# First unit of a float32-split attention kernel: weight stages in other places, keys and queries before the last values, low parts put from ScalarE's queue, Wo split four tiles later

## The reference

```python
q, k, v = X @ Wq, X @ Wk, X @ Wv                    # 16, 8, 8 heads of 64
q = q * cos + rotate_half(q) * sin                  # and k likewise
att = softmax(where(causal, 50 * tanh(q @ k.T / 16 / 50), -inf))
x = layernorm(X + (att @ v) @ Wo)
...                                                 # per-row int8 quantisation of x
x = layernorm(x + ((q8 @ weight.T) * in_scale * w_scale + bias).astype(float16))
```

## Time and profile before

| what | us |
|---|---|
| median of three runs (1493.48 to 1496.95) | 1494.65 |
| the profiled execution | 1498.59 |
| its span in the profile | 1496.8 |
| PE busy in the span | 1327.0 |
| DVE, ACT, POOL busy | 1094.6, 847.4, 379.1 |

### The profile page before, as it was taken

How to read it: one execution, slowest core, us unless ns; L and a number is a source line. 1 busy time by engine, 2 the same in 40 slices (tenths; PEclk the granted TensorE clock), 3 DMA queues, 4 the chain that set the end, 5 groups by cost and what they waited for, 6 DMA issues and landing times.

```text
span 1496.8 us, 17694 instructions
## 1 busy us (share of the span) xinstructions
PE 1327.0 (89%) x5824; PEld 964.5 (64%) x5840; DVE 1094.6 (73%) x1367; ACT 847.4 (57%) x952; POOL 379.1 (25%) x448
## 2 busy tenths in 40 slices
PE   6479999888987999998987999989799799999794
PEld 5356777666665777675755677767576577776462
DVE  4368888782687788885477788878357788888485
ACT  4156777761236777864232877676223486779332
POOL 2231111111462111110265112111136311111275
PEclk9889999998998999999899899999899899999896
DMA  7755445474424345537341444445642244343431
GB/s 281 259 194 153 114 112 133 115 213 158 129 61 105 92 115 133 165 84 222 127 140 50 109 118 124 107 146 149 207 136 79 79 115 107 99 108 105 152 108 42
DMA packets 117038, 196.23 MB, mean 131 GB/s; under 512 B 28498, under 2 KB 70484, under 8 KB 112724
## 3 DMA queue, kind: packets, MB, share of 16 engines
q1 hardware_dynamic: 112340, 186.73, 44.1%
q10 hardware_dynamic: 4608, 8.39, 1.5%
HBM read 89.39 MB, written 38.54 MB: 85 GB/s over the span
## 4 chain that ended last, share of the span: by engine, by line
PE 55%; SPq 14%; DVE 11%; DMA 7%; issue 6%; ACT 3%; POOL 3%; DVEq 0%; ACTq 0%; POOLq 0%
PE ps L720 18%; PE ps L694 13%; PE ps L643 13%; SPq L474 8%; PE ps L757 6%; PE ps L665 4%; SPq L487 3%; DMA d_scratch<-sums 2%; DMA rows<-r_scratch 2%; SPq L465 1%; DMA qk<-work_r 1%; ACT probs L888 1%; DVE probs L1138 1%; DVE stats L1159 1%; SPq L490 1%
## 5 line engine op out<-in xcount | busy, mean ns | idle before, releaser
L720 PE MATMUL ps<-prob_hi,v 128*65 128x512 f32 (+3 forms) x1280 | 415.0, 374 | 5.9 <-DVE prob_lo L1077 5.9
L694 PE MATMUL ps<-qk 128*128 128x512 f32 (+1 forms) x1280 | 326.8, 382 | 71.7 <-DMA qk<-work_r 40.3
L888 ACT ACTIVATE probs<-ps 128x1024 f32<-128x1024 f32 x288 | 293.4, 1019 | 148.6 <-PE ps L694 147.2
L1077 DVE TENSOR_TENSOR prob_lo<-probs,prob_hi 128x1024 fp32r<-128x1024 f32 x288 | 355.6, 1235 | 9.9
L1286 POOL TENSOR_SCALAR_AFFINE_SELECT probs<-probs 128x256 f32<-128x256 f32 (+1 forms) x192 | 144.7, 761 | 805.4 <-ACT probs L893 805.4
L694 PEld LDWEIGHTS ps<-qk 128*128 128x128 f32 x1280 | 230.4, 194 | 137.6 <-issue 39.7
L893 ACT ACTIVATE probs<-probs 128x1024 f32<-128x1024 f32 x288 | 305.7, 1061 | 8.8
L1073 DVE CAST prob_hi<-probs 128x1024 fp32r<-128x1024 f32 x288 | 205.9, 715 | 128.4 <-POOL probs L1286 80.1
L643 PE MATMUL ps<-xT,w_ring 128*128 128x512 f32 x1152 | 291.2, 398 | 1.6 <-DVE v L1022 1.5
L643 PEld LDWEIGHTS ps<-xT,w_ring 128*128 128x128 f32 x1152 | 218.9, 192 | 48.5 <-issue 2.2
L720 PE MATMUL ps<-prob_lo,v 128*65 128x512 f32 (+1 forms) x640 | 238.8, 373 | 0.0
(11 more groups left out here) (77 smaller groups left out, 1041.7 us busy)
## 6 DMA issues: line engine op xcount, KB each, us to landing
qk<-work_r SPq DMA_DIRECT2D x256, 128.0 KB, 2.3
qk<-work_r SPq DMA_DIRECT2D x512, 64.0 KB, 2.0
y_scratch<-sums SPq DMA_DIRECT2D x256, 64.0 KB
wo<-wo_scratch SPq DMA_DIRECT2D x8, 2048.0 KB, 8.0
y_raw<-y_scratch SPq DMA_DIRECT2D x32, 512.0 KB, 3.6
w_ring<-w_scratch SPq DMA_DIRECT2D x15, 1024.0 KB, 5.3
x_raw<-X_T SPq DMA_DIRECT2D x16, 512.0 KB, 5.8
x_in<-X SPq DMA_DIRECT2D x32, 256.0 KB, 2.8
```

The lines of the kernel that those rows point to most:

```text
L694: mm = nc.tensor.matmul(scores[:, g % 2, col:col + REP * w].rearrange("p (h q) -> p h q", h=REP), qk[:, n % 2, i, 2 + part, keys], qk[:, n ...
L720: mm = nc.tensor.matmul(sums_ps[:, :, GQ - w:GQ], v[:, kt, v0:v0 + width], p[:, g % ring, col:col + REP * w].rearrange("p (h q) -> p h q", ...
L888: nc.scalar.activation(probs[:, g % PRING, :], scores[:, g % 2, :], ACT.Tanh, scale=SCORE_SCALE / SOFTCAP).then_inc(capped, 1)
L1077: nc.vector.tensor_tensor(prob_lo[:, g % PRING, :], probs[:, g % PRING, :], prob_hi[:, g % HRING, :].bitcast(F32), ALU.subtract).then_inc( ...
```

## The change

1. Stages: 1 and 3 share one place over `prob_hi` (3 after 1 is stored), 2 lies in the last part of `qk` and the fourth slot of `w_ring`. None lies in `work` now. DVE waits for stage 3 to be stored only before its first `probs_of`.
2. PE multiplies keys and the first queries of unit 0 after six tiles of values, the second queries after all eight. The PSUM banks change so that these don't collide. The weights of stage 0 are split before values 2 and 3.
3. `put` is a function of the engine. Of unit 0, ACT issues the low parts of keys and first queries, SP the rest. ACT rounds the last two tiles of values between and after these puts, and splits stage 3 after them.
4. SP stores stages 2 and 3 between the puts, and loads raw Wo after the last put of unit 0 and after the load of unit 1's query weights.
5. In unit 0 the parts of unit 1's chunks come four, three and two steps later, the splits of Wo four steps later (ACT steps 4 to 7, POOL 5 to 8), its stores three steps later.

```diff
-        stages = [w_ring[:, 0:3, :, :, :]] + [
-            over(f"w_stage{n}", base, [P, 3, 2, KC, P], F32R, skip=skip)[:, :, :, :, :]
-            for n, base, skip in ((1, "qk", 0), (2, "qk", 12 * KB), (3, "work", 4 * KB))]
+        w_stage = over("w_stage", "prob_hi", [P, 3, 2, KC, P], F32R)
+        w_late = over("w_late", "qk", [P, 2, 2, KC, P], F32R, skip=56 * KB)
...
         def chunk_bank(m, x):
-            return (0, 2, PROJ_BANK)[x] if between(m, x) else PROJ_BANK
+            return ((2, 0, PROJ_BANK) if m == 0 else (0, 2, PROJ_BANK))[x] if between(m, x) else PROJ_BANK
-        def v_bank(t):
-            return (PROJ_BANK + t) if t < 2 else t % 2
+        def v_bank(b, t):
+            return t % 2 if t in (2, 3) or (b > 0 and t >= 4) else PROJ_BANK + t % 2
...
-        def turns(u, *steps):
-            return tuple(s + (2, 1, 1)[x] for x, s in enumerate(steps)) if u == UB - 1 else steps
+        def turns(b, u, *steps):
+            later = (2, 1, 1) if u == UB - 1 else (4, 3, 2) if b == u == 0 else (0, 0, 0)
+            return tuple(s + n for s, n in zip(steps, later))
...
+            store_stage(0)
+            store_stage(1)
+            put(sp, 0, 0, 0)
+            store_stage(2)
+            sp.wait_ge(projected, chunks_upto(0, 0))
+            load_wk(1)
+            put(sp, 0, 1, 0)
+            store_stage(3)
+            put(sp, 0, 2, 0)
+            put(sp, 0, 2, 1)
             sp.wait_ge(projected, chunks_upto(0, 2))
             load_wq(1)
+            sp.wait_ge(w_stored[2], 32)
+            sp.dma_start(wo_raw[:, :, :], Wo.rearrange("(k p) n -> p k n", p=P)).then_inc(wo_raw_in, 16)
...
-                        if m == 1 and s == 5:
+                        if m == 1 and s == 8:
                             sp.wait_ge(wo_hi_done, 4)
...
                     if m == 0:
                         pe.wait_ge(w_lo_done, 1)
-                        pe.wait_ge(v_lo_done, rows_upto(0, NT - 1))
+                        pe.wait_ge(v_lo_done, rows_upto(0, (1, 3, NT - 1)[x]))
...
                 if t == 1:
                     turn_tables()
-            for x in range(3):
-                project(0, x, 0, 24)
+                if t == 5:
+                    project(0, 0, 0, 24)
+                    project(0, 1, 0, 24)
+            project(0, 2, 0, 24)
...
+            split_w(2)
+            round_rope(0, 0)
+            put(act, 0, 0, 1)
             round_v(0, 6)
+            round_rope(0, 1)
+            put(act, 0, 1, 1)
             round_v(0, 7)
-            split_w(2)
             split_w(3)
-            for x in range(3):
-                round_rope(0, x)
+            round_rope(0, 2)
...
-                        if b == 0 and u == 0 and s < 4:
-                            split_wo(s)
+                        if b == 0 and u == 0 and 4 <= s < 8:
+                            split_wo(s - 4)
```

More of the change, by code:

```diff
@@ L375, in v_high, with stage @@
             return v[:, t, 0:V_LO].rearrange("p (j e) -> p j e", e=VJ)[:, :, 0:HD]
+        def stage(u, x):
+            if u == 0:
+                return w_ring[:, x, :, :, :]
+            if u == 2:
+                return w_late[:, x, :, :, :] if x < 2 else w_ring[:, 3, :, :, :]
+            return w_stage[:, x, :, :, :]
         def raw_q_half(u, x):
@@ L381, in raw_k_half, with put @@
             return raw_k[:, :, :].rearrange("p k (h x d) -> p k h x d", x=2, d=HD // 2)[:, :, 2 * u:2 * u + 2, x, :]
+        def put(eng, m, x, low):
+            eng.wait_ge(rope_lo if low else rope_hi, chunks_upto(m, x))
+            if m == 1:
+                eng.wait_ge(wo_stored, 32)
+            if m >= 2:
+                eng.wait_ge(scored, unit_scored(m - 2))
+            if m % UB == 1 and m > 1:
+                eng.wait_ge(o_done, rows_upto(m // UB - 1, NT - 1))
+            buf = qk[:, m % 2, :, :, :]
+            for i in range(2):
+                if x == 0:
+                    for half in range(2):
+                        src = work_r[64 * half + 32 * i:64 * half + 32 * (i + 1), place_of(m, x), 1 - low, :].bitcast(F32)
+                        for copy in range(2):
+                            r0 = 64 * copy + 32 * half
+                            eng.dma_start(buf[r0:r0 + 32, i, 2 + low, :].bitcast(F32), src
+                                         ).then_inc(k_put[m % 2][i], 16)
+                else:
+                    cols = slice((x - 1) * HT, x * HT)
+                    for r in range(REP):
+                        h = REP * i + r
+                        for half in range(2):
+                            src = work_r[32 * h:32 * (h + 1), place_of(m, x), 1 - low, half * HT:(half + 1) * HT].bitcast(F32)
+                            r0 = 64 * low + 32 * half
+                            eng.dma_start(buf[r0:r0 + 32, i, r, cols].bitcast(F32), src
+                                         ).then_inc(q_put[m % 2][x - 1][i], 16)
         block = ctx.enter_context(nc.Block())
@@ L444, in load_wv @@
                              wv_scratch[:, :]).then_inc(wv_loaded, 16)
[L447 to L475, removed]
             def put_sums(b, j, c):
@@ L509, in _, with store_stage @@
                          ).then_inc(wv_stored, 16)
-            for u in range(UB):
+            def store_stage(u):
                 sp.wait_ge(w_hi_done, u + 1)
@@ L553, in _ @@
                             load_div(b, 0)
[L554 to L558, removed]
+                        if at := chunk_at(b, u, s, turns(b, u, 5, 10, 14)):
+                            put(sp, *at, 0)
+                        if at := chunk_at(b, u, s, turns(b, u, 6, 11, 15)):
+                            put(sp, *at, 1)
+                        if s == turns(b, u, 0, 0, 12)[2] and m < U:
                             sp.wait_ge(projected, chunks_upto(m, 2))
@@ L1355, in _ @@
                         mask(b, g)
-                        if b == 0 and u == 0 and 1 <= s < 5:
-                            split_wo(s - 1)
+                        if b == 0 and u == 0 and 5 <= s < 9:
+                            split_wo(s - 5)
                 split_y(b, 0)
```

81 lines of the change are left out of this document (42 added, 39 removed).

## The result

The changed kernel takes 1503.09 us (median of 11 runs), the kernel before 1496.76 (11 runs on the same chip). The ratio is 1.0047, 95% interval 1.0032 to 1.0063: 5 to 9 us slower. Forecast were 3.7 us faster and a time of at most 1499.

The account below looks back on a forecast made before the run. SP's put issuing was taken to bound the scores up to step 20: +2.3 (Wo stored later), −5.8 (shorter queue), −0.2 (last wait and rounding) gave −3.7, from 1498.6 to 1494.9, against the median 1491.0; range 1485 to 1499.

Parts of the forecast that it names:

- storing of Wo: Before unit 1's puts: Wo stored at 116.9 instead of 114.6, so these puts start 2.3 later.
- shorter queue: SP's queue in unit 1: 37.7 becomes 31.9, mainly since two of five groups of sums leave it; −5.8.
- What bounds: Start-up to step 20: SP's put issue holds up the scores; step 20 ends on a put, PE is full afterwards.
- I take 0.63: ScalarE's puts in unit 0: 0.63 issue each, as on SP, between bounds of 0.39 and 0.63.
- fourth rival: Unit 0's puts: SP and ScalarE issue in turn at one shared 0.63, step 20 moves −3.7 + 7.7, 1498.6; chance 0.16.
- leave the engines time: Argument against the fourth rival: in SP's put stretch the DMA engines moved only 195 GB/s.
- Wo's landing: Raw Wo's load after unit 0's puts: issued behind query weights at 82.2, about 10.5 to land, there at 93.0.
- the prediction's own signs of being wrong: Step 20 not ended by SP's queue, PE not full after it, or Wo landing over 3 us from 93.
- POOL's side (3.37): POOL's fourth Wo split, behind step 8's mask: 3.37 beside DVE, done at 109.0.
- It isn't the bound: PE from step 2 to 20: step 18 by 135.4, step 20 by 143.6, ahead of SP's queue at 152.7.
- the four cases: Main 1491.0, chance 0.48; cheap issue or fast Wo 1487, 0.17; Wo eats the gain 1494.7, 0.19; queues hinder 1498.6, 0.16.
- Slower: Whole kernel: outcome slower than the kernel before by over about 0.2% (3.0 us); chance 0.17.

Follow-up runs that it names:

- run 5: Changed kernel with GpSimd's low-part splits of Wo left out but for 16 of 512 columns; ratio to the kernel before 1.0018.
- runs 2: Changed kernel with the stage 2 store and unit 1's key load moved in SP's queue behind ScalarE's puts; ratio to the kernel before 1.0028.
- run 8: As versions 7, but ScalarE issues the first queries' low part after rounding the last value tile and splitting stage 3; ratio 0.9856, 1475.5 against 1497.1 us.
- Run 1: Changed kernel with unit 0's sixteen low puts given back from ScalarE to SP; ratio to the kernel before 1.0002.
- run 6: Kernel before with only the new stage places and VectorE's later wait for stage 3, all puts on SP; ratio 0.9976.
- run 3: Changed kernel with raw Wo loaded right after stage 3's store, ahead of the second queries' puts; ratio to the kernel before 1.0031.
- run 4: run 3 with unit 1's parts and Wo's splits and stores back at their old steps in unit 0; ratio to the kernel before 0.9983.
- versions 7: Run 1 with stage 2 and unit 1's keys before all puts, Wo loaded and split early, unit 1's parts at old steps; ratio to the kernel before 0.9903.

## Why the prediction was wrong

Up to step 20 and through the groups behind it, forecast and measurement differ by 10.2 (−3.7 against +6.5 at the mark). Of this SP's queue between the first put of unit 1 and the last makes 5.4, the storing of Wo 2.6, the restart of PE 2.0 and the last wait 0.2. The step that failed is the −5.8 for the "shorter queue": measured were −0.4, since in steps 5 to 8 POOL's splits of Wo slowed VectorE, and SP then stood still for results that came late (run 5).

**What bounds, and up to ScalarE's puts: right.** Step 20 is ended by SP's queue in both kernels, and PE is full after it (94.66 of 94.70). Keys were turned and rounded 0.8 earlier than forecast.

**The price of ScalarE's issue: too low.** "I take 0.63" was for a lone queue. Measured were 0.95 and 0.85 each: value 7 was rounded at 61.9 where 58.3 was forecast, the second queries began at 63.3 for 59.7, and step 2 at 84.2 for 81.1. That falls within the fourth rival's mark (it decides from 0.86 on), but its mechanism, one shared issue of 0.63, is refuted: SP and ScalarE together issued their first sixteen puts from 43.30 to 52.15, 0.55 each, and 64 KB puts on both queues kept nearly the lone price where there was less traffic (runs 2 and 8). Held up were the issues beside full engines, 1.00 busy at 301 GB/s from 49 to 60. I had written that 195 GB/s "leave the engines time", and that stretch lacked the store and the load which the change puts there.

**What a second issuing engine saves.** The Trainium skill, "DMA: Bandwidth & Descriptors", section "Issuing engines are not separate DMA queues", has all issuing engines share the same 16 DMA engines, so that a second one saves only time to initiate. Run 1 goes further: the moved puts were worth −5.4, because they stood ahead of the values' rounding. In run 8, behind it, eight puts moved were worth 5.1 from start to mark, about SP's 5.0 of issue. So the rule is right on what is saved, and "usually small" does not hold for this queue; that run 8's gain is the issue saved rests on one profile of each version.

**Wo's landing: mis-sized.** Forecast 93.0, measured 97.0, 3.0 of it from the later issue and 1.0 from 11.1 to land. That is more than 3 from 93, one of the prediction's own signs of being wrong.

**Step 2 to 20: the failed step, which turned the sign.** The balance is, from the rows of before and after:
- Wo stored: forecast 2.3 later, measured 4.9 (the first keys put of unit 1 at 119.62 against 114.70).
- SP's queue from there to the last low part: forecast 5.8 shorter, measured 0.4 (37.3 against 37.7). The two groups of sums are gone from it, as forecast. But the queue now stood still for ScalarE's sums and for VectorE's low part (1.3 before 134.39, 2.2 before 143.67), and the keys' issues took 1.4 over their price.
- Restart of PE at the lower clock (0.57 for 1.00) after the longer stop: forecast 0, measured 2.0 (the two groups 2.08 and 3.20 against 1.19 and 1.99 in the kernel before).
- Together 4.9 − 0.4 + 2.0 = 6.5, the mark's shift. The first term compares two executions and may be off by the 1.4 by which their starts vary; the other two are lengths within one execution.

The cause behind most of the second item is that I priced VectorE at its undisturbed durations in steps 5 to 8, though edit 5 moves POOL's splits just there, beside VectorE's turn of unit 1's keys. I added the contention to POOL's side (3.37) and none to VectorE's. Run 5 shows it: without POOL's work the same stretch of SP's queue takes 33.6 instead of 37.3, and both stops are gone. Of the 5.4 it thus explains 3.7; the rest is mainly the keys' slow issue, which stays at 1.1 over its price there and whose cause no run isolates. "It isn't the bound" was to leave PE 9 us of slack (step 20 at 143.6, step 18 at 135.4); step 18 came at 147.6. PE still didn't end step 20, but ScalarE's sums and VectorE's chunks hang on it, and SP waits for these. The Trainium skill, "GPSIMD Engine Reference", section "Specifications", says that POOL's SBUF interfaces are shared with VectorE, with contention for instructions in a 2-port mode or with two SBUF inputs. The trace agrees: the subtraction with two SBUF inputs took 3.33 for 1.23, the operation with one of its inputs in PSUM 1.21 as usual. The cast, with one SBUF input, took 2.89 for 0.73; whether it ran in such a mode no trace shows.

None of the four cases reached the time: the slowest was 4.0 above the kernel before, measured were 6.3. "Slower" had a chance of 0.17.

**Which edit cost what.** Edit 1 alone gains 5.5 at the mark (run 6). In the changed kernel ScalarE's share costs 5.4 (run 1), the late Wo load 2.4 (run 3), POOL's splits beside VectorE 2.9 (run 5) and the late steps, given an early load, 6.9 (run 4 against 3). These can't be added up: runs 1, 3 and 5 start from the changed kernel, run 4 from run 3, run 6 from the kernel before. Edit 2, keys ahead of the last values, was never run alone; that it pays in versions 7 and 8 is argued from their start, not shown apart from the other edits.

## What to carry to other kernels

A lead won at the start is worth only what is left of it at the first step that another chain also reaches; here a weight's load, split and store decided it. Put later, they ate the lead; left in their place (run 6) or moved up (runs 7 and 8), most of it or more came through. Before DMAs are moved to a compute engine's queue, look what stands behind them in that engine's order: sixteen such puts cost 5.4 ahead of the rounding, and eight of them gained 5.1 behind it. Price a moved operation with its new neighbours, on both engines of a pair that slow each other down and beside the transfers of the new place.

## What was not expected of the hardware

- A put's issue depends on the traffic: 0.63 on SP, 0.66 on ScalarE beside it, 0.77 (ScalarE) and 0.71 (SP) for 128 KB puts on both queues at once, 0.85 to 0.95 on ScalarE with 2 MB of stores and loads beside, the engines 1.00 busy, and 0.89 on SP beside full engines with no second queue (run 6).
- Beside POOL's 128x1024 subtraction, VectorE's cast of the same size took 2.89 for 0.73, and its subtraction 3.33 for 1.23; an operation from PSUM and one tile of SBUF was not slowed.
